# A windowed-attention block on one core: projection from 64-row halves, and the layer norm's aggregation behind the addition of the table

## The reference, cut to what matters

```python
q, k, v = (shuffle_invert(conv3(xw, w, b), 2) for ...)   # windows of 16x16: 64 tokens of 128
q, k, v = ln(q), ln(k), ln(v)                            # over the 128 features of a token
attn = softmax(q @ k.T * SCALE + bias_table[RPI])        # 8 heads of 16, per window
out = (attn @ v) @ proj_w.T + proj_b
xr = xw + pixel_shuffle(out, 2)
y = xr + conv3(gelu(conv3(xr, c1w, c1b)), c2w, c2b)
return x + y
```

## Time and profile before

| what | us |
|---|---|
| median of 3 runs | 828.27 (827.14 to 828.51) |
| the profiled execution, its own time | 826.6 |
| its span, first to last instruction | 824.6 |
| PE busy in it | 743.8 |
| DVE busy | 657.1 |
| ACT busy | 601.3 |
| POOL busy | 492.6 |

### The profile page before, as it was taken

The page is one execution under the profiler, slowest core; times in us unless marked ns, Lnnn a source line. Parts: engine busy times, 40 slices in busy tenths (PEclk is TensorE's granted clock), DMA queues, the critical chain, the costliest instruction groups (busy, mean ns, idle before and its releaser), DMA issues.

```text
span 824.6 us, 17835 instructions
## 1 busy us (share of the span) xinstructions
PE 743.8 (90%) x5704; PEld 539.0 (65%) x5704; DVE 657.1 (80%) x2141; ACT 601.3 (73%) x1287; POOL 492.6 (60%) x1041
## 2 busy tenths in 40 slices
PE   0479999999899999989799999999999999998988
PEld 0247777677556777767555777777655677777753
DVE  6559888897759888887967988889775988887675
ACT  1399889767467898876647988976837789878640
POOL 5467778642457788763336777874244778785210
PEclk9999999999999999999999999999999999999999
DMA  7111421000113161000101342100101213000002
GB/s 258 58 36 53 140 94 58 2 1 17 43 59 100 33 233 41 20 1 2 57 26 56 110 139 97 58 1 2 44 16 66 96 30 133 1 2 2 1 1 103
DMA packets 17661, 47.23 MB, mean 57 GB/s; under 512 B 2080, under 2 KB 2720, under 8 KB 17568
## 3 DMA queue, kind: packets, MB, share of 16 engines
q1 hardware_dynamic: 17568, 46.09, 16.2%
HBM read 37.69 MB, written 8.39 MB: 56 GB/s over the span
## 4 chain that ended last, share of the span: by engine, by line
PE 55%; ACT 16%; DVE 12%; issue 8%; POOL 7%; DMA 0%; SPq 0%; POOLq 0%; ACTq 0%; DVEq 0%
PE y_ps L1006 16%; PE o_bank L1070 5%; PE s_ps L1045 5%; ACT ot L819 5%; PE ox_ps L1077 4%; PE pt_ps L1058 4%; PE y_ps L975 4%; POOL ln_rs L719 3%; DVE ln_st L536 3%; ACT qk_n L851 3%; PE ox_ps L1115 3%; PE o_bank L1115 3%; PE pt_ps L1115 3%; PE s_ps L1115 3%; PE t_ps L1031 2%
## 5 line engine op out<-in xcount | busy, mean ns | idle before, releaser
L732 POOL TENSOR_TENSOR sc<-sc,mx 128x512 f32<-128x512 f32 x128 | 133.7, 1044 | 60.8 <-DVE mx L563 60.8
L851 ACT ACTIVATE qk_n<-y_ps,ln_nr,ln_rs 128x128 f32<-128x128 f32 x256 | 104.4, 465 | 80.2 <-POOL ln_nr L722 80.2
L1006 PE MATMUL y_ps<-w_hi,x_hi 128*128 128x192 f16 (+1 forms) x512 | 147.6, 288 | 0.0
L1006 PE MATMUL y_ps<-w_hi,x_lo 128*128 128x192 f16 (+1 forms) x512 | 147.3, 288 | 0.0
L1006 PE MATMUL y_ps<-w_lo,x_hi 128*128 128x192 f16 (+1 forms) x512 | 147.2, 288 | 0.0
L536 DVE BATCH_NORM_STATS2 ln_st<-y_ps 128x6 f32<-128x128 f32 x384 | 88.8, 287 | 68.0 <-PE y_ps L1006 66.7
L1070 PE MATMUL o_bank<-v_bd,pt 128*128 128x66 f32 x1024 | 129.1, 269 | 4.5 <-DVE on L584 4.3
L1070 PEld LDWEIGHTS o_bank<-v_bd,pt 128*128 128x128 f32 x1024 | 124.4, 192 | 6.1 <-DVE pt L570 5.3
L719 POOL TENSOR_TENSOR ln_rs<-ln_ve,neg_half 128x3 f32<-128x3 f32 x128 | 113.4, 886 | 10.7
L866 ACT ACTIVATE sc<-sc 128x512 f32<-128x512 f32 x128 | 83.0, 649 | 36.4 <-POOL sc L732 36.4
L715 POOL TENSOR_TENSOR ln_ve<-ln_mv,eps_y 128x3 f32<-128x3 f32 x128 | 35.1, 274 | 120.2 <-DVE ln_mv L541 120.0
(11 more groups left out here) (181 smaller groups left out, 1606.3 us busy)
## 6 DMA issues: line engine op xcount, KB each, us to landing
xs<-in_x_sh_dram SPq DMA_DIRECT2D x32, 576.0 KB, 4.3
xst<-in_x_al_dram SPq DMA_DIRECT2D x16, 512.0 KB, 8.2
xf<-in_x_al_dram SPq DMA_DIRECT2D x32, 256.0 KB, 5.4
out_dram<-xf SPq DMA_DIRECT2D x32, 256.0 KB, 2.0
wst<-in_wqkv_dram SPq DMA_DIRECT2D x1, 768.0 KB, 4.1
w1s<-in_w_dram SPq DMA_DIRECT2D x1, 256.0 KB, 8.5
w2s<-in_w_dram SPq DMA_DIRECT2D x1, 256.0 KB, 8.5
biasS<-in_bias_t_dram SPq DMA_DIRECT2D x1, 256.0 KB, 9.4
```

The costliest lines, as they stand in the source:

```text
L732: pool.tensor_tensor(sc[i % 4][:, :, :, :], sc[i % 4][:, :, :, :], mx[i % 2][:, :, :].unsqueeze(2).to_broadcast([P, HP, TOK, 2]), ALU.subt ...
L851: ins = act.activation(qk_n[j][:, t, :].rearrange("p (h y x) -> p h y x", h=HEADS, y=2), by_head(y_ps[j][:, E * t:E * (t + 1)]), ACT.Identity,
L1006: ins = pe.matmul(y.rearrange("p (t e) -> p t e", t=3)[:, :, cols], xx[r % 2][:, s, a % 2, 2 * TS * (a // 2):2 * TS * (a // 2 + TS)], ww[: ...
```

## The change

**The projection.** The four `ot` copies of a row become one of 128 x 512 with no rearrangement. The window sits then in the partition (64 rows each) and the half of the features in the columns, so the projection weights `projg` are kept as two halves of 64 features, each held twice, and the projection is four matmuls of 64 rows and 256 columns, two windows times two halves, the second half added to the first. It writes, for rows 0 to 5, the free back halves of the two `s_ps` banks; for row 6 `ox_ps` and `t_bank`; for row 7 `ox_ps` and `pt_bank`. It waits therefore for the addition of the table of the same step (`biased`), and the scores of the next step wait for the addition to `xr`. `ox_ps` is free earlier: `by_feature` now does one pair in every step, where before the step of the projection did none and the next one two. The addition to `xr` is one instruction for rows 0 to 5, two for rows 6 and 7.

**The aggregation.** In the steps that have both scores of a pair i and stats of pair i+5 (0 to 26, 27 steps of an image) the one-column copy goes, the addition of the table waits for the stats in its place, and the three aggregations follow the addition. In steps -5 to -1 the old order stays.

**The set-up.** `projw` is twice as wide, its largest value is taken over both halves, `projg` is scaled in two operations, and the product for the projection's offset is two small matmuls.

```diff
-                    v.wait_ge(ln_stats, p0 + (m + 1))
-                    v.tensor_copy(wait_slot[:, :], vec[:, 0:1])
-                    for t in range(3):
-                        ins = v.bn_aggr(ln_mv[m % 2][:, t, :], ln_st[m % 2][:, t, :])
-                    ins.then_inc(ln_moments, 1)
+                    if not has(i):
+                        v.wait_ge(ln_stats, p0 + (m + 1))
+                        v.tensor_copy(wait_slot[:, :], vec[:, 0:1])
+                        ln_aggregate(m)
...
+                    if has(i + 5):
+                        v.wait_ge(ln_stats, p0 + (i + 6))
                     v.tensor_tensor(sc[i % 4][:, :, :, :].rearrange("p (a h) k w -> p a (h k w)", a=2),
                                     s_ps[:, :, 0:256], biasS[:, :, :], ALU.add).then_inc(biased, 1)
 
+                if has(i) and has(i + 5):
+                    ln_aggregate(i + 5)
...
-                    rows = xr[:, TS * r:TS * (r + 1), :].rearrange("p i (w j) -> p w i j", w=NWIN)
-                    v.tensor_tensor(rows, rows, ox_ps[:, :].rearrange("p (w i j) -> p w i j", w=NWIN, i=TS),
-                                    ALU.add).then_inc(xr_added, 1)
+                    rows = xr[:, TS * r:TS * (r + 1), :].rearrange("p i (m w j) -> p w (i m) j", w=2, j=TS)
+                    if r < 6:
+                        v.tensor_tensor(rows, rows, s_ps[:, :, 256:512].rearrange("p w (n j) -> p w n j", j=TS),
+                                        ALU.add).then_inc(xr_added, 1)
+                    else:
+                        for w in range(2):
+                            ins = v.tensor_tensor(rows[:, w, :, :], rows[:, w, :, :],
+                                                  proj_bank[r][w].rearrange("p (n j) -> p n j", j=TS), ALU.add)
+                        ins.then_inc(xr_added, 1)
...
-                    for w in range(2):
-                        for par in range(2):
-                            ins = act.activation(
-                                ot[r % 2][64 * par:64 * par + 64, :].rearrange("p (m w t) -> p m w t", w=2, t=TOK)[:, :, w, :],
-                                ox_ps[64 * w:64 * w + 64, :].rearrange("p (m a t) -> p m a t", a=2, t=TOK)[:, :, par, :],
-                                ACT.Copy)
-                    ins.then_inc(ot_copied, 1)
+                    act.activation(ot[r % 2][:, :], ox_ps[:, :], ACT.Copy).then_inc(ot_copied, 1)
...
+                    if i % 4 == 1 and 9 <= i < 32:
+                        pe.wait_ge(xr_added, r0 + (i - 9) // 4 + 1 + ADD0)
...
-                    pe.matmul(ox_ps[:, :], projg[:, :], ot[r % 2][:, :], start=True, stop=True).then_inc(
-                        proj_done, 1)
+                    if r < 6:
+                        pe.wait_ge(biased, p0 + (i + 1))
...
+                    for par in range(2):
+                        for w in range(2):
+                            half = slice(64 * w, 64 * w + 64)
+                            ins = pe.matmul(proj_bank[r][w].rearrange("p (i m j) -> p i m j", i=TS, m=NPAIR),
+                                            projg[half, par, :],
+                                            ot[r % 2][half, :].rearrange("p (m a i j) -> p a i m j", m=NPAIR, a=2, i=TS)[
+                                                :, par, :, :, :], start=par == 0, stop=par == 1)
+                    ins.then_inc(proj_done, 1)
...
-                if i % 4 == 1:
+                if i == PAIRS + 1:
                     by_feature(i - 5, p0, r0)
-                if i % 4 > 0:
+                if i != PAIRS:
                     by_feature(i - 4, p0, r0)
```

More of the change, by code:

```diff
@@ L42 @@
 GN_BOUND = float(IMG)
-GQ, BQ, GK, BK, GV, BV, PB, C1B, EVEN, ODD, C2B, EVEN2, ODD2, WIN0, WIN1 = range(15)
-NVEC = 15
+GQ, BQ, GK, BK, GV, BV, PB, C1B, EVEN, ODD, C2B, EVEN2, ODD2, WIN0, WIN1, GVP, GVP1, BVP, BVP1 = range(19)
+NVEC = 19
 T1R = 5
@@ L87, in conv_attention @@
         biasS = sb("biasS", [P, 2, HP * TOK])
-        projw = sb("projw", [P, P])
-        projg = sb("projg", [P, P])
+        projw = sb("projw", [P, 2, P])
+        projg = sb("projg", [P, 2, P])
         w1s = sb("w1s", [P, 4, P])
@@ L262, in conv_attention @@
         c2_bank = [c_ps[3], c_ps[2], pt_bank, o_bank[:, :], ox_ps[:, :], pt_bank, o_bank[:, :], ox_ps[:, :]]
+        proj_bank = [[s_ps[:, w, 256:512] for w in range(2)] for r in range(6)]
+        proj_bank += [[ox_ps[:, 0:256], t_bank[:, 0:256]], [ox_ps[:, 0:256], pt_bank[:, 0:256]]]
         c2_in = {-5: (0,), -4: (1,), -3: (2,), -2: (3,), -1: (4,), 0: (5,), 1: (6,), 2: (7,)}
@@ L404, in largest @@
                 v.wait_ge(loaded_consts, 16 * 4)
-                v.tensor_reduce(amax[:, A_PROJ:A_PROJ + 1], projw[:, :], AX.X, ALU.max, apply_absolute_value=True)
+                v.tensor_reduce(amax[:, A_PROJ:A_PROJ + 1], projw[:, :, :], AX.XY, ALU.max, apply_absolute_value=True)
                 v.tensor_reduce(amax[:, A_C1:A_C1 + 1], w1s[:, :, :], AX.XY, ALU.max, apply_absolute_value=True)
@@ L427, in conv_scales @@
                 link(v.reciprocal(y_down[:, :], y_up[:, :]))
-                v.tensor_scalar(projg[:, :], projw[:, :], vec[:, GV:GV + 1], up[:, 0:1], ALU.mult, ALU.mult)
+                for par in range(2):
+                    v.tensor_scalar(projg[:, par, :], projw[:, par, :], vec[:, GVP + par:GVP + par + 1], up[:, 0:1],
+                                    ALU.mult, ALU.mult)
                 v.wait_ge(setup_pe, 1)
@@ L518, in border, with ln_aggregate @@
                 ins.then_inc(h_border, 1)
+            def ln_aggregate(m):
+                for t in range(3):
+                    ins = v.bn_aggr(ln_mv[m % 2][:, t, :], ln_st[m % 2][:, t, :])
+                ins.then_inc(ln_moments, 1)
             def step(i, p0, h0, r0, rr0, row0, b=None, followed=False, last=None):
@@ L943, in mean_of_proj @@
                 pe.wait_ge(loaded_consts, 16 * 4)
-                pe.matmul(pt_ps[:, 0, 0:1], projw[:, :], vec[:, BV:BV + 1], start=True, stop=True).then_inc(setup_pe, 1)
+                for par in range(2):
+                    ins = pe.matmul(pt_ps[:, 0, 0:1], projw[0:64, par, :], vec[0:64, BVP + par:BVP + par + 1],
+                                    start=par == 0, stop=par == 1)
+                ins.then_inc(setup_pe, 1)
             def mean_of_phases(b, n, of):
@@ L983, in by_feature @@
                     pe.wait_ge(normed, p0 + (m + 1))
-                    if m % 4 == 0:
+                    if m == PAIRS - 4:
                         pe.wait_ge(xr_added, r0 + m // 4 + ADD0)
+                    elif m % 4 == 0 and m >= 4:
+                        pe.wait_ge(ot_copied, r0 + m // 4)
                     pe.transpose(ox_ps[:, P * (m % 4):P * (m % 4 + 1)], on[m % 4][:, :, :, :].rearrange(
@@ L1076, in step @@
                     pe.wait_ge(ot_copied, r0 + (r + 1))
-                    pe.matmul(ox_ps[:, :], projg[:, :], ot[r % 2][:, :], start=True, stop=True).then_inc(
-                        proj_done, 1)
+                    if r < 6:
+                        pe.wait_ge(biased, p0 + (i + 1))
+                    if r == 6:
+                        pe.wait_ge(qkt_done, h0 + PAIRS // 2)
+                    if r == 7:
+                        pe.wait_ge(pt_copied, p0 + PAIRS)
+                    for par in range(2):
+                        for w in range(2):
[5 more added lines that the diff above has]
+                    ins.then_inc(proj_done, 1)
                 if i == PAIRS + 4:
@@ L1081, in step @@
                         c1(b, t)
-                if i == 5 and b > 0:
+                if i == 4 and b > 0:
                     pe.wait_ge(y_ready, (b - 1) * T2N + T2N + 1)
-                if i % 4 == 1:
+                if i == PAIRS + 1:
                     by_feature(i - 5, p0, r0)
-                if i % 4 > 0:
+                if i != PAIRS:
                     by_feature(i - 4, p0, r0)
@@ L1104, in c2 @@
                 elif t == 2:
-                    pe.wait_ge(pt_copied, b * PAIRS + PAIRS)
+                    pe.wait_ge(xr_added, b * NROW + NROW + ADD0)
                 elif t == 3:
@@ L1237, in _lay_out @@
     bias_t = np.ascontiguousarray(bias_t).reshape(P, 2, HP * TOK)
-    proj_t = np.ascontiguousarray(g["proj_w"][e_m][:, r_v].T)
+    proj_t = g["proj_w"][e_m][:, r_v].T.reshape(2, 64, P)
+    proj_t = np.ascontiguousarray(np.concatenate([proj_t, proj_t], axis=1).transpose(1, 0, 2))
+    by_par = [np.tile(g[n][r_v].reshape(2, 64), 2) for n in ("gv", "bv")]
     even = (e // HD % 2 == 0).astype(np.float32)
@@ L1242, in _lay_out @@
     vecs = np.stack([g["gq"][f_nat], g["bq"][f_nat], g["gk"][f_nat], g["bk"][f_nat], g["gv"][r_v], g["bv"][r_v],
-                     g["proj_b"][e_m], g["c1b"][e_ph[2]], even, 1 - even, g["c2b"][e_ph[2]], even2, 1 - even2, first, 1 - first], axis=1)
+                     g["proj_b"][e_m], g["c1b"][e_ph[2]], even, 1 - even, g["c2b"][e_ph[2]], even2, 1 - even2, first, 1 - first,
+                     *by_par[0], *by_par[1]], axis=1)
```

## The result

The changed kernel takes 843.19 us (median; 838.54 to 843.79) against 828.24 before: a ratio of 1.017, interval 1.013 to 1.021. It is slower by 15 us, where 829.3 was predicted, with a range that ended at 833.2. The profiled execution has a span of 841.3, 16.7 more than before, and a mean granted clock of 0.982 instead of 0.991.

A forecast was written before the change was run, and what follows sets the result against it. PE was taken as the bound, busy 743.8 of 824.6 us. Rows and tails -4.16, later heads +4.05, image 0 +0.9 and set-up +0.2 gave +1.0 on 826.6, so 827.6; 829.3 against the median, range 823.0 to 833.2.

The forecast's parts named there:

- A waiting row: Rows 1 to 4 of an image, where PE waits for `ot`: 0.64 later, 0.95 sooner, 0.10 mode change, -0.21 each.
- The wait of the heads: PE's wait ahead of the transposes, attributed to step 3 of each later head: from 1.20 to some 2.5 us.
- Step 27: Called step 26 there: transposes for k of the last pairs wait 0.64 beyond 0.95; +0.35 an image after row 5's wait.
- The two new waits that were costed at nothing: Projection waiting for `biased`, scores waiting for the addition to `xr`: both covered; at most 0.69 a row if the latter's cover failed.
- image 0: First image, no results in its head: late aggregation in step 1 costs PE +0.9, the set-up on DVE +0.2.
- the head of images 1 to 3: Step 3 aggregation goes behind `sum_input`, `result` and the addition, 2.0 later; PE loses 1.35 each, +4.05 in three images.
- delay passes whole: Rival: the heads' aggregation delays, 2.0 in three images and 2.6 in image 0, reach PE undiminished; 832.9, chance 0.17.
- the drain: PE draining at 128/64-row mode changes: 0.10 per waiting row; rival, open at both ends of 32 projections, 837, chance 0.06.
- The tail's -0.70: Image end: shorter `ot` copies let the convolution tile at 413.13 come at some 412.42; -0.70 an image, bounds 0.5 and 0.95.

The follow-up runs named there:

- the kernel with the filled waits: The change plus identity transposes keeping PE at work ahead of the transposes of steps 5 (18) and 27 (14); 830.41 us, ratio 1.002.
- the head-only kernel: The change, with the aggregation behind the addition of the table only in steps 0 to 3; 824.74 us, ratio 0.996.
- the projection alone: The change with the aggregation put back to its old place, behind its copy and ahead of the table's addition; 810.83 us, ratio 0.979.
- The aggregation alone: The kernel before with only the aggregation moved behind the addition of the table, old projection kept; 865.64 us, ratio 1.045.
- The kernel with the longer wait: The kernel before plus two unneeded ACT copies in step 3 of the three later heads, lengthening PE's wait; 842.59 us, ratio 1.016.

## Why the prediction was wrong

The mechanisms on the engines were right, and in the rows they were sized well. The `ot` copy was taken at 0.60 and is 0.597. The matmuls run in pairs, 1.13 as said. The aggregation was to end 0.64 later, and does by 0.67. A waiting row was to be shorter by 0.21; rows 2 and 3 are shorter by 0.24 each. The wait of the heads was to grow from 1.20 by 1.35; it grew by 1.06, and by 0.49 at a second place, the softmax's transposes, which I had not counted. Step 27 was to wait 0.64 more and waits 0.78 more. The two new waits that were costed at nothing show nothing: the scores have no idle time ahead of them in the whole run, and what ends the idle time ahead of the projections is `ot`. (A slip without effect: 331.01 and 0.69 make 331.70; 331.74 is the start of the copy behind the stats, and the scores decide there.)

Without the loss of clock behind these waits the time is near the forecast of 829.3: the kernel with the filled waits takes 830.4. That it is so near is partly luck. In its profiled execution, 1.8 us above its median, the heads cost 0.6 each more than forecast, image 0 cost 4.0 more and the tails got no shorter; against that the rows gained 1.2 more, and so did the stage from pair 28 to 31, where the kernel before had lost clock in image 0.

The step that failed is the price of a wait. The term "the head of images 1 to 3" put PE's loss equal to the idle time, +1.35 each. It measured +5.1 each: 1.9 as waits (40.3 with the clock full, in two kernels, against 38.4) and 3.2 as matmuls at half clock after them. The 1.9 is 0.55 above the term, for the second wait; the 3.2 were not in the sum at all. Step 27 was priced in the same way and lost clock too, in images 1 and 3. Taken alone these two would move the forecast by three times 3.75 and by some 3 us, to about 844.

The trace of the kernel before showed that such a price exists. Around the wait of 1.63 for the projection of row 4 in image 0, windows of 2 us read

```profile
160.00:162.00 2.00, 1.81 (x7) 1.00 (x8) 0.85 (x3) 1.97 (x6) 1.92 (x5) 0.85 0.00 0
162.00:164.00 2.00, 2.00 (x9) 1.09 (x8) 0.64 (x2) 2.00 (x6) 0.21 (x1) 0.50 0.01 4
164.00:166.00 2.00, 2.00 (x18) 1.55 (x17) 1.58 (x8) 0.01 (x1) 0.41 (x2) 0.79 0.00 0
```

and at the tails of images 0 to 2 there are windows at 0.50 to 0.85 too; the last projection of image 1 took 2.07 where the others took 1.13. It did not show when the price is due: behind the same wait of 1.64 in images 1 (356.97) and 2 the clock held. I kept the 2.07 in the sum as a constant of the place, and asked of no other wait whether it would come to the same. The rival "delay passes whole" had the right place and sign but again the wait's own length as price, 832.9, so the range could not reach.

The Trainium skill, page "TensorE: Matmul & The Clock Gate", Part 1, says that the clock's default is the throttled one and that activity releases it. These runs agree as far as they go: behind the waits of the heads the granted clock is 1.00 where PE was kept at work in them (830.4), and falls to 0.50 in all three heads where the same wait was idle (843.2). It also held once behind an idle wait of 2.26, in image 1 of the head-only kernel. Of the drain that the Trainium skill, page "TensorEngine Tiling (Array Packing)", section Key Properties, states, little is seen: with the projection alone a row without any wait takes 17.38, where before 18.02 held 0.59 of idle time, so 17.4 without it.

The tail's -0.70 was in good part not the price of the `ot` copies. With the projection alone the stage from pair 31 on is 69.5 instead of 70.3 in images 0 and 1, and 72.7 instead of 73.4 in the last; but in image 2 it is 69.52 instead of 69.58. There the last projection of the kernel before ran at full clock, and the tile of the first convolution already stood 0.16 behind the end of `xr_lo`:

```profile
606.27 1.13 POOL L704 TENSOR_TENSOR xr_lo<-xr,xr_hi 128x512 f16<-128x512 f32 x1 [3.14 <-ACT xr_hi L800]
...
607.56 0.30 PE L975 MATMUL y_ps<-xr_hi,w_hi 128*128 128x325 f16 x1
```

In image 1 it stood 0.88 behind it (412.25 and 413.13), after matmuls at half clock. The 0.70 that I read there as room was that half clock. Under the change the stage is 70.2 where the clock holds (images 0 and 2) and 71.8 where step 27 lost it (image 1). The 70.2 is 0.7 more than with the projection alone: step 27 waits 1.73 instead of 1.04, the addition to `xr` comes as much later, and DVE has no idle time ahead of it.

Image 0 lost 3.1 to its pair 12, where I had 1.1. From pair 4 on it lost 1.7, where I had 0.9, and PE shows a wait there that I had not counted, ahead of the convolution of pair 8:

```profile
64.11 0.34 PE L1018 MATMUL y_ps<-b_parts,ones_b 96*128 96x384 bf16 x1 [1.64 <-POOL x_lo L716]
```

It is gone with the old order in steps 0 to 3 (the stage takes 32.1 then, instead of 33.9). The other 1.4 had come by pair 4, behind a stretch of half clock at 38 to 44 us that the kernel before does not show in its profiled execution. The aggregation alone, whose set-up is the old one, shows such a stretch and 1.0 there; the head-only kernel, with the new set-up, shows none and 0.2. The kernel with the longer wait, whose image 0 is the old one unchanged, shows such a stretch too and 1.5. So it differs from execution to execution and is not the set-up. What decides it stays open, and so does why the clock falls behind a 2.26 us wait in image 2 and not in image 1 of one execution.

## What to carry to other kernels

An idle stretch of TensorE can have two prices, its length and the matmuls behind it at half clock; here the second was almost twice the first where it was due, so before moving work onto a chain that TensorE waits for, look in the windows for the places where the clock already falls, and ask which wait would become the next. Two edits on one chain can hide each other: the projection's gain of 17 us and the aggregation's loss of 32 on top of it looked like one change that loses 15, and only running them apart showed that half of it was worth keeping. Saving the 0.15 us instruction gave nothing where DVE had idle time, and the 0.67 by which the aggregation moved was paid in full by the rows that waited for it.

## What had not been expected of the hardware

The `sum_input` of step 3 takes 1.64 in the changed kernel (260.75), beside POOL's subtraction of 1.04 from 260.80; in the kernel before it took 0.72 (260.76, with only POOL's short operations beside it), and `result` followed at 261.58. In the new order the two meet, and the `sum_input` is 0.92 longer. That is about what the delay of the aggregation has over the forecast: 3.2, less the 0.4 by which the step is late, is 2.8, where I had 2.0. The kernel before shows the same elsewhere: its `sum_input` at 249.81 and 255.14 take 1.45 and 1.34 beside POOL's `x_lo` of 1.16 each.
